# A decoder block on one core: the odd heads of a long convolution run in three passes on halves that are made ahead

## What is computed

```
k = v = ctx;  q = layernorm(x)              # each (8 batches, 256 = 32 heads x 8, 512 positions)
kv  = einsum('bhil,bhjl->bijhl', k_, v_)    # per head: the 64 products of its 8 rows with its 8 rows
y   = irfft(rfft(kv) * rfft(ssm_kernel))    # a causal convolution along the positions, one kernel for each head
out = y + kv * D
out = einsum('bijhl,bhil->bjhl', out, q_)   # the 64 results, weighted with the 8 rows of q and summed to 8
```

## Time and profile before

| | |
|---|---|
| time, median of 3 | 863.47 us |
| the profiled execution | 862.55 us, of which its span is 859.8 |
| busy: PE, PEld | 840.5 us (98%), 702.5 us (82%) |
| busy: DVE, ACT, POOL | 542.5 us (63%), 377.8 us (44%), 440.9 us (51%) |
| granted clock of TensorE, mean | 0.995 |
| transfers | 113.42 MB, mean 132 GB/s |

### The profile page before, as it was taken

How to read it: one execution, slowest core, us unless ns; L and a number is a source line. 1 busy time by engine, 2 the same in 40 slices (tenths; PEclk the granted TensorE clock), 3 DMA queues, 4 the chain that set the end, 5 groups by cost and what they waited for, 6 DMA issues and landing times.

```text
span 859.8 us, 14213 instructions
## 1 busy us (share of the span) xinstructions
PE 840.5 (98%) x4354; PEld 702.5 (82%) x4354; DVE 542.5 (63%) x851; ACT 377.8 (44%) x608; POOL 440.9 (51%) x435
## 2 busy tenths in 40 slices
PE   8999999999999999999999999999999999999994
PEld 7888888889877777778887778888888888888884
DVE  6766767675657777888769875544555544555431
ACT  5313322333133533442652255555555555655552
POOL 1203223331068899884622344666656666656653
PEclk9999999999999999999999999999999999999998
DMA  8601001100026543440210397988998889999866
GB/s 287 216 25 19 32 25 36 37 12 13 1 63 197 166 129 110 124 131 18 93 63 7 119 334 158 225 204 200 193 193 220 204 218 188 191 207 216 205 115 84
DMA packets 54420, 113.42 MB, mean 132 GB/s; under 512 B 10416, under 2 KB 14256, under 8 KB 54256
## 3 DMA queue, kind: packets, MB, share of 16 engines
q1 hardware_dynamic: 37360, 72.49, 26.5%
q0 software_dynamic: 17024, 40.48, 25.8%
HBM read 82.28 MB, written 30.66 MB: 131 GB/s over the span
## 4 chain that ended last, share of the span: by engine, by line
PE 90%; DVE 5%; issue 2%; POOL 1%; ACT 1%; DMA 0%; POOLq 0%; DVEq 0%; ACTq 0%
PE PS L206 20%; PE PS L208 20%; PE PS L207 20%; PE PS L217 17%; PE PS L1645 4%; PE PS L704 2%; PE PS L695 2%; PE PS L633 1%; PE PS L1582 1%; PE PS L1572 1%; PE PS L1612 1%; PE PS L1581 1%; PE PS L1564 1%; DVE KV L491 0%; PE PS L638 0%
## 5 line engine op out<-in xcount | busy, mean ns | idle before, releaser
L206 PE MATMUL PS<-QY_rounded,wh 128*128 128x512 f32 (+1 forms) x376 | 153.2, 407 | 0.0
L208 PE MATMUL PS<-QY_rounded,wl 128*128 128x512 f32 (+1 forms) x376 | 145.7, 387 | 0.0
L1360 POOL DMA_INDIRECT out_y<-QY,idy x72 | 114.5, 1590 | 44.3 <-ACT QY L1454 33.0
L207 PE MATMUL PS<-QY_rounded,wh 128*128 128x512 f32 (+1 forms) x312 | 120.0, 385 | 0.0
L1916 DVE TENSOR_TENSOR hTl<-hh,hTh 128x512 fp32r<-128x512 f32 (+1 forms) x39 | 27.5, 706 | 107.6 <-ACT hTh L1435 106.2
L1337 POOL DMA_INDIRECT xg<-xs_d,idx x64 | 77.2, 1207 | 28.8 <-issue 15.1
L208 PEld LDWEIGHTS PS<-QY_rounded,wl 128*128 128x128 f32 x376 | 70.6, 188 | 15.1
L217 PE MATMUL PS<-qER,Tz 128*128 128x288 f32 x320 | 81.1, 407 | 0.5 <-DVE QY L1062 0.4
L217 PE MATMUL PS<-prod,Tz 128*128 128x288 f32 x320 | 80.5, 406 | 0.2 <-DVE term L1045 0.2
L206 PEld LDWEIGHTS PS<-QY_rounded,wh 128*128 128x128 f32 x376 | 71.0, 189 | 11.1
L1454 ACT ACTIVATE QY<-PS,WPOS 128x512 f32<-128x512 f32 x76 | 52.5, 690 | 55.0 <-PE PS L208 44.5
(11 more groups left out here) (238 smaller groups left out, 1903.1 us busy)
## 6 DMA issues: line engine op xcount, KB each, us to landing
ws<-in_gu_w SPq DMA_DIRECT2D x38, 512.0 KB
ws<-in_dn_w SPq DMA_DIRECT2D x20, 512.0 KB, 5.6
C<-in_ctx SPq DMA_DIRECT2D x32, 256.0 KB, 2.7
Tz<-kpad_d SPq DMA_DIRECT2D x32, 256.0 KB, 3.2
xs_d<-xn SPq DMA_DIRECT2D x16, 256.0 KB, 2.0
out_y<-X SPq DMA_DIRECT2D x16, 256.0 KB
X<-in_x SPq DMA_DIRECT2D x1, 3072.0 KB, 17.5
xn<-in_xT SPq DMA_DIRECT2D x5, 512.0 KB, 3.3
```

Source lines behind the costliest of these rows:

```text
L206: pe.matmul(out_, lh, rh, start=first, stop=False)
L207: pe.matmul(out_, lh, rl, start=False, stop=False)
L208: return pe.matmul(out_, ll, rh, start=False, stop=last)
L1360: nc.gpsimd.indirect_dma_start(out=out, out_offset=bass.IndirectOffsetOnAxis(ap=idy[:, t:t + 1], axis=0), in_=yo[:, t], in_offset=None, co ...
```

## The change

The 15 odd heads from 3 to 31 are no longer convolved in plain float32, but in three passes on halves. The parts of it:

- The padded kernel is also written in two halves (`kpad_hl_d`): GpSimd makes them at the start.
- For each batch from 2 to 6 GpSimd makes the products of three odd heads in the attention's loop (`products_ahead`), ScalarE makes their high halves (`high_ahead`), GpSimd the low ones (`low_ahead`), and SyncE stores both (`prod_hl_d`). That makes 5 x 3 = 15 heads. They use `prod[0]` and a part of QY that is still free, so that mean and factor of the normalisation go to `Tz[0]` rather than to QY, and head 0's products are made behind the loop.
- In the convolution SyncE loads the four halves of an odd head (two of the Toeplitz tile, two of the products) into one of two buffer sets (`load_halves`), and TensorE runs 10 x 3 passes (`convolve_halves`).
- The even heads now take turns with both sets of `C2`, `Tz` and `prod`. GpSimd makes one head's products in a pair of heads instead of two.
- Of the shared expert's weights GpSimd makes the low part in 6 pieces of 512 elements instead of 3 of 1024.

```diff
+            for j in range(2):
+                sp.wait_ge(kpad_done, j + 2)
+                sp.dma_start(kpad_hl_d[j], kpad_hl[j].bitcast(F32)).then_inc(kpad_out, 16)
+            sp.wait_ge(kpad_out, 16 * KPADS)
+            load_context(sp, 3, 0)
+            load_context(sp, 5, 1)
...
+            def ahead_batch(b, last=False):
+                m = b * AHEAD + (1 - DIRECT * AHEAD)
+                made = b * AHEAD_STEP - DIRECT * AHEAD_STEP
+                highs = b * AHEAD - DIRECT * AHEAD
+                sp.wait_ge(ahead_hi, highs + 1)
+                store_half(0, m, ahead_high, hi_out)
+                ahead_context(m + 2, 0)
+                sp.wait_ge(ahead, made + AHEAD_MADE[1])
...
+                sp.wait_ge(ahead, made + AHEAD_LOW[0])
+                store_half(1, m, ahead_prod[0], lo_out)
+                sp.wait_ge(ahead_hi, highs + 2)
+                store_half(0, m + 1, ahead_high, hi_out)
+                sp.wait_ge(ahead, made + AHEAD_LOW[1])
+                store_half(1, m + 1, ahead_prod[1], lo_out)
...
+                sp.wait_ge(ahead_hi, highs + 3)
+                store_half(0, m + 2, ahead_high, hi_out)
+                sp.wait_ge(ahead, made + AHEAD_LOW[2])
+                store_half(1, m + 2, ahead_prod[0], lo_out)
...
+            with sp.Fori(DIRECT, B - 1) as b:
+                turned_batch(b)
+                ahead_batch(b)
+            turned_batch(B - 1)
+            ahead_batch(B - 1, last=True)
...
+            def products_ahead(j, s):
+                k = AHEAD_BUF[j]
+                pool.wait_ge(c2_in[k], s * (32 - 16 * k) + (16, 16, 32)[j])
+                if j == 0:
+                    wait_apart(pool, lo_out, s * (16 * AHEAD))
+                a = C2[k][:]
+                if k == 0:
+                    o = prod[0][:].rearrange("p c b n -> p (c b) n")
+                    for half in range(2):
+                        shifted = bass.AP(tensor=a.tensor, offset=a.offset + 2 * half, ap=[a.ap[0], a.ap[1], [1, 2], [1, CD]])
+                        nc.gpsimd.tensor_tensor(o[:, :, 2 * half * CD:2 * (half + 1) * CD].rearrange("p a (s j) -> p a s j", s=2),
+                                                a[:, :, 0:CD].unsqueeze(2).broadcast_to([P, LB, 2, CD]), shifted,
+                                                ALU.mult).then_inc(ahead, 1)
+                    nc.gpsimd.tensor_tensor(o[:, :, 4 * CD:], a[:, :, 0:4], a[:, :, 4:8], ALU.mult).then_inc(ahead, 1)
...
+            def low_ahead(j, s):
+                o = ahead_prod[AHEAD_BUF[j]]
+                wait_apart(pool, ahead_hi, s * AHEAD + j + 1)
+                if j == 1:
+                    wait_apart(pool, lo_out, s * (16 * AHEAD) + 16)
+                nc.gpsimd.tensor_tensor(o.bitcast(F32R), o, ahead_high, ALU.subtract).then_inc(ahead, 1)
+
+            wait_apart(pool, kpad_out, 16 * KPADS)
+            wait_apart(pool, w_lo, W_PARTS)
             with pool.Fori(2, B - 1) as b:
                 rstd(pool, 0, b + 1, mv[0][:, :, 1])
+                s = b - (DIRECT - 1)
+                products_ahead(0, s)
+                products_ahead(1, s)
+                low_ahead(0, s)
                 wait_apart(pool, xt_mr_in, 32 * (b - 1))
                 for t in range(TPB):
                     part = xz[:, :, t * P:(t + 1) * P]
@@ -320,7 +424,12 @@
                     wait_apart(pool, z_done, 2 * TPB * (b - 2) + t + 1)
                     nc.gpsimd.tensor_tensor(part, part, mean_rstd[:, t:t + 1, :, 1].broadcast_to([P, DC, P]),
                                             ALU.mult).then_inc(z_done, 1)
+                low_ahead(1, s)
+                products_ahead(2, s)
                 rstd(pool, 1, b - 1)
+                low_ahead(2, s)
+            wait_apart(pool, lo_out, 16 * (CH // 2 - 1))
+            products(pool, 0, 0)
...
+            def high_ahead(b, j):
+                n = b - (DIRECT - 1)
+                wait_apart(act, ahead, n * AHEAD_STEP + max(AHEAD_MADE[j], AHEAD_LOW[j - 1] if j else 0))
+                wait_apart(act, hi_out, n * (16 * AHEAD) + 16 * j)
+                act.activation(ahead_high.bitcast(F32R), ahead_prod[AHEAD_BUF[j]], ACT.Copy).then_inc(ahead_hi, 1)
+
             def step(b, first=False, last=False):
+                made_ahead = not (isinstance(b, int) and b < DIRECT - 1) and not last
                 q_evac(b, first)
                 if last:
+                    wait_apart(act, hi_out, 16 * (CH // 2 - 1))
+                    wait_apart(act, lo_out, 16 * (CH // 2 - 1))
                     qy_evac(b - 2)
+                if made_ahead:
+                    high_ahead(b, 0)
                 k_evac(b)
                 if not first:
                     a_hi(b - 1)
+                if made_ahead:
+                    high_ahead(b, 1)
                 if isinstance(b, int) and b < DIRECT - 1:
                     x_hi(b + 1)
                 elif not last:
                     z_hi(b + 1)
                     qy_evac(b - 2)
+                    high_ahead(b, 2)
...
+                def load_halves(m):
+                    k = m % 2
+                    for j, (t, dst) in enumerate(((TzHi[k], odd_h[k]), (TzLo[k], odd_l[k]))):
+                        src = bass.AP(tensor=kpad_hl_d.tensor, offset=(j * CH + 2 * m + 1) * (KPAD + 1), ap=[[1, P], [1, D]])
+                        sp.dma_start(t[:], src).then_inc(halves_in[k], 16)
+                        sp.dma_start(dst[:].rearrange("p c b n -> p (c b n)"), prod_hl_d[j, m]).then_inc(halves_in[k], 16)
+
...
+                sp.wait_ge(hi_out, 16 * (CH // 2 - 1))
+                sp.wait_ge(lo_out, 16 * (CH // 2 - 1))
+                sp.wait_ge(v_ps, TPB * B)
+                sp.wait_ge(o_ps, TPB * B)
+                load_halves(1)
+                load_halves(2)
+                next_heads(0)
...
-                with pe.Fori(1, stream_head(0) // 2) as i:
-                    for k in range(2):
-                        convolve(pe, i, k)
+                def convolve_halves(m, k, loads, behind=None):
+                    pe.wait_ge(halves_in[k], 64 * loads)
+                    pe.wait_ge(y_read[1], 2 * m)
+                    for c in range(DC):
+                        o = PS[:, DC + c].rearrange("p (b n) -> p b n", n=YGAP)[:, :, 0:NPAIR]
+                        for r in range(c + 1):
+                            w = slice((c - r) * P, (c - r + 1) * P)
+                            mm = three_pass(pe, o, TzHi[k][:, w].bitcast(F32R), TzLo[k][:, w].bitcast(F32R), odd_h[k][:, r].bitcast(F32R), odd_l[k][:, r].bitcast(F32R), r == 0, r == c)
+                        if behind is not None and c == DC - 1:
+                            mm = behind()
+                        mm.then_inc(conv_ps[1], 1)
+
+                with pe.Fori(0, stream_head(0) // 4) as j:
+                    for k in range(1, 3):
+                        convolve(pe, 2 * j + k, k - 1, used=j + 2)
+                        convolve_halves(2 * j + k, k % 2, j + 1)
```

More of the change, by code:

```diff
@@ L45 @@
 DIRECT = 3
+AHEAD = 3
+KPADS = 3
 WARM = 10
@@ L136, in decoder_program @@
         kpad_done, kpad_out = sem("kpad_done"), sem("kpad_out")
+        kpad_hl = [a[:].rearrange("p c s -> p (c s)")[0:CH, 0:KPAD + 1] for a in (aTh, aTl)]
+        ahead, ahead_hi = sem("ahead"), sem("ahead_hi")
+        hi_out, lo_out = sem("ahead_hi_out"), sem("ahead_lo_out")
+        halves_in = [sem(f"halves_in{k}") for k in range(2)]
+        NPROD = B * NPAIR
+        late = QY[:].rearrange("p c b s -> p c (b s)")[:, :, (B - 3) * S:]
+        ahead_high = late[:, :, 0:NPROD]
+        ahead_prod = [prod[0][:].rearrange("p c b n -> p c (b n)"), late[:, :, NPROD:2 * NPROD]]
+        AHEAD_BUF = (0, 1, 0)
+        AHEAD_MADE, AHEAD_LOW, AHEAD_STEP = (3, 8, 13), (9, 10, 14), 14
         tz_in = [sem(f"toeplitz_in{k}") for k in range(2)]
@@ L220, in convolve @@
                     mm = behind()
-                mm.then_inc(conv_ps[k], 1)
+                mm.then_inc(conv_ps[odd], 1)
         @block_.sync
@@ L749, in _ @@
             step(B - 1, last=True)
-            convolve(pe, 0, 1, (3,))
+            convolve(pe, 0, 1, (3,), odd=1)
             att_t(B - 1, bank=4)
@@ L759, in _ @@
                 pe.wait_ge(x1_done, TPB * (B - 1) + t + 1)
-                warm((5, 3)[t], bank=4 + t)
+                for _ in range((5, 3)[t]):
+                    pe.matmul(PS[:, 4 + t], WH[:, 3, 0, 0:P], WH[:, 3, 0], start=True, stop=True)
                 pe.wait_ge(xns[1], TPB * (B - 1) + t + 1)
@@ L895, in decoder_program @@
         term = [sb2(f"term{k}", [P, CD // 2, LB, CD, 2]) for k in range(2)]
+        odd_h, odd_l = ([sb2(f"odd_{n}{k}", [P, DC, B, NPAIR]) for k in range(2)] for n in ("high", "low"))
+        TzHi, TzLo = ([sb2(f"Tz_{n}{k}", [P, D]) for k in range(2)] for n in ("high", "low"))
         q2_done, term_behind, reduced = sem("q2_done"), sem("term_behind"), sem("reduced")
@@ L928, in _ @@
                     sp.dma_start(out[rows], zrow[:, 0:D]).then_inc(zero_out, 16)
```

(9 more changed lines are left out.)

169 lines of the change are left out of this document (102 added, 67 removed).

## The result

The changed kernel took 889.18 us in the median (888.94 to 889.77), the kernel before 863.19 (860.99 to 865.67): a ratio of 1.031, interval 1.029 to 1.032, so 26 us slower. The forecast was 892 us. Of all executions timed here one of the kernel before (1065 us) and one of the kernel with all three edits (1040 us) ran at a granted clock of 0.751 and are left out of every figure. The changed kernel's profiled execution has a span of 886.8 us, 27.0 more than before.

What follows compares the result with a forecast made beforehand. TensorE, 90% of the chain that ended last, bounds the kernel; 32.6 us added in the attention plus 8.1 at the convolution's start minus 12.0 gained make 28.7 on 862.55: 891.3, forecast as 892 us, range 884 to 902.

Steps and rivals of the forecast that it cites:

- The gain of a head: Convolution: an odd head takes 4.05 us instead of 4.88, 0.80 gained with small gaps; 15 heads give 12.0, at most 19.
- Turns in the attention: Attention: VectorE and GpSimd wait for each other's operations on a shared port; five steps lose 32.6 us together.
- the 32 to 35 named as a sign of being right: Attention: steps of 32 to 35 us would show the forecast right, steps of 28 us would show it wrong.
- The third low half: Attention: queued ahead of `ln_norm`, it holds that for 2.6 us; the normalisation's factor is ready at 10.6 instead of 7.2.
- the first rival: Attention: GpSimd doesn't hold line 447 (`ln_norm`), so a step grows by 4.7 us, 9 less in all: 883 us; chance 0.23.
- The normalisation's start: Attention: GpSimd's normalisation starts 21.7 us into a step instead of 14.4 and lasts 5.1.
- "I count 0" for the clock in the attention: Attention: TensorE's clock may fall in each step's wait before `t2`; counted 0, at most 1.4 x 5 = 7 us.
- The wait before the projection of k: Attention: TensorE waits 0.7 us for `att_norm` before projecting k, in a step with a third low half ahead.
- Head 2's tile: Convolution's start: the tile queues behind two heads' halves, 6.7 us late, plus 1.4 for the fallen clock: 8.1.
- ScalarE's copies and the transfers at 0: Attention: three ScalarE copies a step cost 0; SyncE's 6 stores and 3 loads cost 0, at most 1 us a step.
- The fourth case: Convolution: transfers can't keep up; at 200 GB/s a pair takes 11.1 us instead of 8.9, 33 on top: 925; chance 0.04.
- The faster rival: Attention: `z_lo` and `x_add` end at most 1.2 us later, so the gain stays: 851.5 or 859.6 us; chance 0.18.

Runs made afterwards that it cites:

- the kernel with all three edits: Changed kernel with low halves in four pieces, the third low half behind ln_norm, Toeplitz tiles of heads 2 and 4 issued earlier; fifteen heads: 868.6 us, ratio 1.008.
- the kernel with both tiles first: Changed kernel with SyncE's issues reordered: head 2's Toeplitz tile, halves of head 3, head 4's tile, halves of head 5: 879.7 us, ratio 1.021.
- The kernel without GpSimd's work: Changed kernel with GpSimd's products and low halves in the attention cut to one column; copies, stores and loads stay: 881.8 us, ratio 1.022.
- the memsets: Changed kernel with GpSimd's products and low halves in the attention replaced by memsets of the same tiles, written twice: 881.7 us, ratio 1.022.
- the ten heads: Changed kernel with ten heads made ahead, five in one fp32 pass, low halves waiting for z_lo and ln_norm, tiles first: 852.0 us, ratio 0.988.
- the kernel with pieces: Changed kernel with each low half made by four GpSimd operations of 288 elements instead of one of 1152: 877.5 us, ratio 1.018.

## Why the prediction was right, step by step

- **The gain of a head** was right: 3.98 us for an odd head, 4.05 forecast. The sum of 12.0 measured 11.1 to the last reduction (the kernel with both tiles first agrees: from `att` to the last reduction 163.8 us against 174.9), because the four heads 19 to 25 are paced by VectorE; the other eleven gained about 0.9 each. I priced all fifteen alike and had not looked for what paces those pairs. 1.2 of it is lost again behind the last head.
- **Turns in the attention** was the right cause. The kernel without GpSimd's work takes all of it away, the memsets show that it is the reads, and the ten heads show that the same kind of work in other places costs nothing. The memsets also show where it bites. By the prediction's own path a normalisation that starts at 17.0 ends the step at 17.0 + 5.1 + 0.6 + 0.6 + 1.2 + 3.0 = 27.5 if nothing holds `z_lo`, and the memset kernel's step of 28.2 agrees; the low half that holds `z_lo` is what makes it long. Its size, 32.6 forecast and 27.8 measured, came out near by luck, from two errors of opposite sign: `x_add` came 3.2 us a step too late in the forecast, and the clock's part was left out. The steps measured +6.0, 5.5, 6.2, 3.1 and 7.0, where I had 5 and four times 6.9; the fourth step, 30.95 us, is below the 32 to 35 named as a sign of being right.
- **The third low half** was over-priced. I had `ln_norm` start 1.04 us behind `att`'s end and the factor ready at 10.6. VectorE runs ahead of TensorE in the slow steps: `ln_norm` starts 0.7 us before that end (127.83 against 128.54), and the factor ends at 7.8. Its place is worth 3.2 us by experiment, and 0.5 where the low halves are in pieces; the first rival had priced it at 9. (That rival also counts 5.7 us for the normalisation where the forecast counts 5.1; with 5.1 it gives 881, not 883.)
- **The normalisation's start** was late, but less than foreseen: at 17.8 in the step instead of 21.7 (before 14.4), in part for the same reason. `x_add` ends at 28.6 instead of 31.8.
- **"I count 0" for the clock in the attention** was wrong as a term: from `x_add`'s end (155.83 + 1.27 = 157.10) to `att`'s (158.98 + 3.56 = 162.54) are 5.4 us where I had 3.0. Over the five steps, from the start of `t2` to the end of `att`, the lower clock makes 7.2 us, just what the prediction had named as the most. How much of it reaches the total is not shown: part of it is what lets VectorE run ahead (1.7 us, from +1.04 to -0.7), so that this error and that of the third low half go together.
- **The wait before the projection of k**, 0.7 us forecast, was 0.6 once in all, not once a step: hidden.
- **Head 2's tile** was right: 6.8 us late (6.7 forecast), and its clock 2.3, where 1.4 was forecast from ten matmuls at the start of the program. By those two rows it is 3.89 - 10/6 x 1.63 = 1.2, and a whole head of 20 pays more. Both tiles first gives 9.5 back.
- **ScalarE's copies and the transfers at 0** were right: without GpSimd's operations the steps are 27.85 us with all copies and stores in place. The fourth case (transfers too slow in the convolution) did not come: pairs of 8.83 us without a wait.
- **The faster rival** was wrong for this kernel, but not far: its condition, that `z_lo` and `x_add` end where they did, is exactly what the ten-head kernel meets, and that one is 10.4 us faster.

## What to carry to other kernels

An engine that is idle for half of a step isn't free time: ask at which moments a long GpSimd operation that reads SBUF would lie over a VectorE operation with two SBUF inputs, and make it wait for the end of that one. Here 5.3 us of low halves in each of five steps cost 24.5 us in one place and nothing to be seen in another. Where a ring of transfers goes in order, issue the small tile that is needed next before the megabytes needed later; for TensorE a wait costs its length and then, where the clock falls, about 2 us more for the head behind it (1.7 and 2.3 here). And a head, tile or pass made faster gains only where TensorE sets the pace; look at each stretch for who does, before multiplying.

## What the runs showed of the hardware

- A tensor_scalar of VectorE is held also by a GpSimd memset: 965 and 1133 ns instead of 421 and 544 in the loop, where two-input operations beside the same memsets took the 681 and 905 ns of the kernel before.
- The hold ends with the instruction: four operations of 288 elements, back to back, let VectorE in between, one of 1152 does not. `z_lo`'s pair fell from 4.13 to 2.32 us. The split costs GpSimd 0.9 to 1.3 us a low half (4.45 and 3.96 against 3.13 and 3.06) and still won 11.7 us.
- What a wait of TensorE costs afterwards can't be read from its length. One of 2.26 us before a head made that head 1.7 us longer, one of 7.1 us made it 2.3 longer. Before `t2` a wait of 2.05 us was followed by the lower clock in one step of the kernel with pieces (`t2` 1.94 us) and not in a step of the changed kernel (1.06 us). With all three edits the clock stayed up behind four waits of 2.7 to 3.2 us and fell behind a fifth of 3.2.
- Leaving part of the data out changed which experts the tokens chose, and with it the experts' stage by 18.7 us. In a kernel whose work depends on data such an experiment is read from the stages ahead of that choice.
